# Values on quarters of the array in a first attention layer, and a new order of issue around the sixth and seventh steps of a second

## Time and profile before

| | us |
|---|---|
| median of 3 runs | 925.53 |
| lowest, highest | 922.88, 928.38 |
| the profiled execution | 926.4 |
| its span, first to last instruction | 924.6 |
| PE busy in it | 881.2 (95%) |
| DVE, ACT, POOL busy | 513.5, 511.7, 374.0 |

### The profile page before, as it was taken

One profiled execution on the slowest core, in us unless ns is written; L12 is line 12 of the kernel. 1 busy time (PEld: TensorE's weight loads), 2 busy tenths in 40 slices (PEclk: granted clock), 3 DMA queues, 4 the chain that ended last, 5 costly groups with the idle time before them and its releaser, 6 DMA issues.

```text
span 924.6 us, 20158 instructions
## 1 busy us (share of the span) xinstructions
PE 881.2 (95%) x6773; PEld 764.1 (83%) x6774; DVE 513.5 (56%) x1257; ACT 511.7 (55%) x1450; POOL 374.0 (40%) x530
## 2 busy tenths in 40 slices
PE   6989999999999999999999987999999999999996
PEld 4567777777777779999999986899999999987653
DVE  4534434444445764434434447877777776666466
ACT  4576777777775244443343462655655555552565
POOL 3173444444443234455454551534434443443000
PEclk9999999999999799999999998999999999999998
DMA  9000000420002466777777813000000000000002
GB/s 267 1 1 2 1 1 2 146 72 1 0 2 80 138 240 234 244 245 258 232 262 246 252 61 89 25 23 13 12 23 11 12 1 2 1 1 0 1 1 91
DMA packets 36673, 76.18 MB, mean 82 GB/s; under 512 B 4941, under 2 KB 22721, under 8 KB 36481
## 3 DMA queue, kind: packets, MB, share of 16 engines
q1 hardware_dynamic: 32865, 65.11, 21.6%
q0 software_dynamic: 3744, 10.23, 3.3%
HBM read 66.02 MB, written 9.31 MB: 81 GB/s over the span
## 4 chain that ended last, share of the span: by engine, by line
PE 88%; DVE 4%; DMA 3%; issue 2%; ACT 1%; POOL 1%; SPq 0%; DVEq 0%; POOLq 0%
PE banks L1542 14%; PE banks L546 14%; PE banks L548 13%; PE banks L547 13%; PE banks L584 8%; PE banks L595 7%; PE banks L574 5%; PE banks L444 3%; PE banks L1827 2%; PE banks L515 1%; PE banks L1838 1%; PE banks L1832 1%; PE banks L1820 1%; PE banks L1532 1%; DMA region_a<-in_L_ffn_b 1%
## 5 line engine op out<-in xcount | busy, mean ns | idle before, releaser
L1098 ACT ACTIVATE region_a<-banks,negmax 128x154 f32<-128x154 f32 (+1 forms) x384 | 161.7, 434 | 29.3 <-DVE negmax L890 26.6
L1542 PE MATMUL banks<-region_b,region_a 128*128 128x128 f32 x1248 | 146.7, 276 | 1.5 <-ACT region_b L1578 1.4
L1542 PEld LDWEIGHTS banks<-region_b,region_a 128*128 128x128 f32 x1248 | 142.7, 192 | 3.2 <-ACT region_b L1578 1.7
L1242 POOL TENSOR_TENSOR region_a<-region_a,recip 128x640 f32<-128x640 f32 x64 | 80.3, 1255 | 137.4 <-DVE recip L894 137.4
L1205 POOL TENSOR_TENSOR region_a<-region_a,recip 128x512 f32<-128x512 f32 x64 | 66.7, 1042 | 134.3 <-DVE recip L894 94.9
L890 DVE TENSOR_REDUCE negmax<-banks 128x4 f32<-128x616 f32 (+1 forms) x128 | 100.5, 785 | 26.9 <-PE banks L574 14.2
L1633 DVE SCALAR_TENSOR_TENSOR region_b<-banks,region_a,region_b 128x128 f32<-128x128 f32 x156 | 43.9, 343 | 106.7 <-PE banks L1542 99.6
L584 PE MATMUL banks<-ident,region_a 128*128 128x128 f32 x640 | 95.0, 279 | 3.2 <-DVE pT_low L901 1.6
L584 PEld LDWEIGHTS banks<-ident,region_a 128*128 128x128 f32 x640 | 72.5, 141 | 16.6 <-issue 11.6
L546 PE MATMUL banks<-xT_high,Wq_high 128*128 128x256 f32 x256 | 77.8, 304 | 4.1 <-DVE xT_low L882 2.1
L1080 ACT CAST pT_high<-banks 128x640 fp32r<-128x640 f32 x64 | 44.4, 694 | 64.9 <-PE banks L584 64.9
(11 more groups left out here) (293 smaller groups left out, 2344.5 us busy)
## 6 DMA issues: line engine op xcount, KB each, us to landing
region_a<-in_L_ffn_W SPq DMA_DIRECT2D x39, 1024.0 KB
W<-in_L_ffn_W SPq DMA_DIRECT2D x1, 4096.0 KB, 17.9
W<-y_rows SPq DMA_DIRECT2D x16, 256.0 KB, 2.8
out<-x SPq DMA_DIRECT2D x8, 256.0 KB, 2.2
x<-in_x SPq DMA_DIRECT2D x1, 1536.0 KB, 13.1
region_b<-in_L_xattn_Wq SPq DMA_DIRECT2D x1, 1024.0 KB, 8.7
region_b<-in_L_xattn_Wo SPq DMA_DIRECT2D x1, 1024.0 KB, 13.6
xn_rows<-region_b SPq DMA_DIRECT2D x1, 1024.0 KB, 4.4
```

The lines of the kernel that those rows point to most:

```text
L1098: e = act.activation(into, source, ACT.Exp, bias=negmax[:, n % 2, u:u + 1], accum_out=sums[:, n % 2, u:u + 1])
L1242: pool.tensor_tensor(probs1[:, n % 2], probs1[:, n % 2], rc, ALU.mult).then_inc(sem("p_norm"), 1)
L1542: mm = pe.matmul(banks[:, 2 * r + part, m * P:(m + 1) * P], W1[r][:, k, cols], xgT[:, r, k, :], start=(k == 0), stop=(k == DK - 1))
```

## The change

For the first layer (L0):

- the values of a whole group are issued at the even step, and none at the odd one. Keys beyond 128 are no longer multiplied with zero rows: the four products (two heads' halves, two chunks) take 64 rows by 64 columns each, a quarter of the array, and the two row halves write to different banks, 5 and 6, columns 128 to 383 (`o0_ps`);
- ACT copies the group from the banks to SBUF (`o0T`), and DVE makes both high and low part from there. PE waits for `o0_copied` in place of `o2_sb`, and, as bank 5 is shared with the fifth transposed block, before that fifth transpose at odd steps; before the values it waits until ACT has copied this step's transposes;
- both output products lie in one bank, side by side in bank 7, and `add_y` for both comes at step 5;
- the next pair's rows are transposed to `o0_ps`, without a wait for `y_done`; the fifth transpose of step 6 waits for `xt2_sb`; `y_done` is awaited ahead of the queries.

For the second layer (L1):

- `pe_pair_x`, with its wait for `y_done`, comes behind `next_scores(6)` instead of ahead of it; ACT and DVE take its copies at the start of step 6;
- `values(6)` is issued ahead of the queries of step 6, and `values(7)` ahead of `next_scores(7)` and the queries of step 7.

```diff
+        o0_ps = banks[:, 5:7, P:P + PAIR]
...
-        def pe_pair_probsT(pe, L, n):
+        def pe_pair_probsT(pe, L, n, groups_copied=None, rows_split=None):
             row = normed if L is L0 else probs_row[:, n % 2]
             for m in range(5):
+                if m == 4 and groups_copied is not None:
+                    pe.wait_ge(sem("o0_copied"), groups_copied)
+                if m == 4 and rows_split is not None:
+                    pe.wait_ge(sem("xt2_sb"), rows_split)
...
+        def pe_group_values(pe, g, b):
+
+            V = V0[b].bitcast(F32)
+            for u in range(2):
+                for i in range(2):
+                    pe.matmul(o0_ps[64 * i:64 * i + 64, u, :], V[:, 2 * g + u, 128 * i:128 * i + 64], p0T[:, g % 2, 2 * u + i, :],
+                              start=True, stop=False)
+            for i in range(2):
+                for u in range(2):
+                    rows = slice(64 * u, 64 * u + 64)
+                    mm = pe.matmul(o0_ps[64 * i:64 * i + 64, u, :], V[rows, 2 * g + u, 192 + 64 * i:256 + 64 * i],
+                                   p0T[rows, g % 2, 4, :], start=False, stop=True)
+            mm.then_inc(sem("o2_ps"), 1)
...
+                if L is L0 and r == 0 and c % 2 == 0:
+                    pe.wait_ge(sem("o2_sb"), groups_done - (NC - 2 - c) // 2)
...
                 def values(n):
                     s = 8 * i + n
+                    if L is L0:
+                        if n % 2 == 0 and not (first and n in (0, 2)):
+                            pe.wait_ge(sem(probs_turned), s)
+                            if not (first and n == 4):
+                                pe.wait_ge(sem("o0_copied"), group + n // 2 - 2)
+                            pe_group_values(pe, (n // 2 - 2) % 4, before if n < 3 else batch)
+                        return
...
                 values(5)
-                if not last:
+                if not last and L is L0:
+                    pe.wait_ge(sem("pt2_high"), 8 * i + 5)
+                    pe.wait_ge(sem("xn_ready"), 2 * i + 4)
+                    pe_pair_x(pe, L)
+
+                next_scores(6)
+                if not last and L is L1:
                     if first:
                         pe.wait_ge(sem("q2_sb"), g0 + 4)
                     else:
                         pe.wait_ge(sem("y_done"), t0 + 2 * i)
                     pe.wait_ge(sem("xn_ready"), t0 + 2 * i + 4)
                     pe_pair_x(pe, L)
-
-                next_scores(6)
                 transposes(6)
...
+                if L is L1:
+                    values(6)
                 if not last:
                     pe.wait_ge(sem("xt2_sb"), x0 + i + 2)
+                    if L is L0:
+                        if first:
+                            pe.wait_ge(sem("q2_sb"), 4)
+                        else:
+                            pe.wait_ge(sem("y_done"), 2 * i)
                     pe_pair_q(pe, L, 0)
-                values(6)
+                if L is L0:
+                    values(6)
 
                 transposes(7)
...
+                if L is L1:
+                    values(7)
                 next_scores(7)
                 if not last:
                     pe.wait_ge(sem("q2_sb"), g0 + 4 * i + 5)
                     pe_pair_q(pe, L, 1)
-                values(7)
+                if L is L0:
+                    values(7)
...
             def o_rest(g, group):
                 high, low = oT_parts[L.index]
                 part = slice(2 * g, 2 * g + 2)
+                if L is L0:
+                    dve.wait_ge(sem("o0_copied"), group + 1)
+                    dve.tensor_copy(high[:, part, :], o0T).then_inc(sem("o2_high"), 1)
                 dve.wait_ge(sem("o2_high"), g0 + group + 1)
-                dve.tensor_tensor(low[:, part, :], o_ps.rearrange("p (u n) -> p u n", u=2),
+                dve.tensor_tensor(low[:, part, :], o0T if L is L0 else o_ps.rearrange("p (u n) -> p u n", u=2),
                                   high[:, part, :].bitcast(F32), ALU.subtract).then_inc(sem("o2_sb"), 1)
...
+                    if L is L1 and n == 6 and not last:
+                        pair_x_rest(i + 2)
                     if not (first and n == 0):
                         probsT_rest((n - 1) % 8, s - 1)
+                    if L is L0 and n % 2 == 1 and not (first and n in (1, 3)):
+                        o_rest((n // 2 - 2) % 4, 4 * i + n // 2 - 2)
...
-                    if n in (3, 5) and not first:
+                    if n in (3, 5) and not first and L is L1:
                         add_y(dve, L, 2 * i + n // 2 - 3, n // 2 - 1, misc_ps[:, 0:D])
-                    if n == 5 and not last:
+                    if n == 5 and not first and L is L0:
+                        dve.wait_ge(sem("y_ps"), 2 * i)
+                        for q in range(2):
+                            add_y(dve, L, 2 * i + q - 2, q, misc_ps[:, q * D:(q + 1) * D])
+                    if L is L0 and n == 5 and not last:
                         pair_x_rest(i + 2)
...
             def o_high(g, group):
                 act.wait_ge(sem("o2_ps"), g0 + group + 1)
+                if L is L0:
+                    if not (isinstance(group, int) and group == 0):
+                        act.wait_ge(sem("o2_sb"), group)
+                    act.copy(o0T, o0_ps).then_inc(sem("o0_copied"), 1)
+                    return
...
+                    if L is L1 and n == 6 and not last:
+                        x_high(i + 2)
                     if not (first and n == 0):
                         probsT_high((n - 1) % 8, s - 1)
```

More of the change, by code:

```diff
@@ L665, in transposes @@
                             pe.wait_ge(sem(probs_turned), s - 1)
-                        pe_pair_probsT(pe, L, (n - 1) % 8)
+                        turned = L is L0 and n % 2 == 1 and not (first and n < 5)
+                        pe_pair_probsT(pe, L, (n - 1) % 8, 4 * i + n // 2 - 1 if turned else None,
+                                       i + 2 if L is L0 and n == 6 and not last else None)
                 def next_scores(n):
@@ L712, in emit @@
                 transposes(3)
-                if not first:
+                if not first and L is L0:
+                    pe_pair_out(pe, L, 1, misc_ps[:, D:2 * D], range(0, 4), 4 * i, True)
+                elif not first:
                     pe_pair_out(pe, L, 0, misc_ps, range(4, NC), 4 * i)
@@ L718, in emit @@
                 transposes(4)
-                if not first:
+                if not first and L is L0:
+                    pe_pair_out(pe, L, 0, misc_ps, range(4, NC), 4 * i)
+                elif not first:
                     pe.wait_ge(sem("y_done"), t0 + 2 * i - 1)
@@ L1015, in emit @@
                         pair_q_rest(4 * i + n - 1, n - 6)
-                    if n % 2 == 0 and not (first and n in (0, 2)):
+                    if L is L1 and n % 2 == 0 and not (first and n == 0 or first and n == 2):
                         o_rest((n // 2 - 2) % 4, 4 * i + n // 2 - 2)
```

78 lines of the change are left out of this document (41 added, 37 removed).

## The result

The changed kernel took 932.39 us (median of 20 runs, 929.99 to 938.05), the kernel before beside it 927.31 (20 runs, 922.88 to 934.02). The ratio is 1.0063 with a 95% interval of 1.0048 to 1.0079: some 6 us slower. The forecast was 933.0. The profiled execution of the changed kernel has a span of 931.6 us, against 924.6 before.

The account below looks back on a forecast made before the run. PE was taken to bound both attention loops, idle only 1.2 of 189.0 and 3.6 of 228.0 us. First layer -4.3 and second +11.7 gave +7.4 on 926.4: 933.8, 933 for the median; range 920 to 944.

Parts of the forecast that it names:

- values(7) waits for the output group: Second layer, step 7: ACT copies queries before the output group, so PE stalls 1.85 us in each pair.
- Second layer, queries of step 0: Second layer: queries of step 0 wait for the low part of step 7's queries, a stall of 0.66 us.
- What goes there: Second layer: waits for y_done (0.7) and xt2_sb (0.25) vanish, together -0.95 us for each of 6 pairs.
- The layer: Second layer's sum: net +1.56 per pair, six pairs +9.4, first pair +2.3, last pair 0: +11.7 us.
- The group on quarters: First layer: a group's values take 1.58 us instead of 2.03, four quarters at once; 30 groups give -13.5 us.
- The rival of two at a time: First layer: quarters run only two at a time, 2.00 us per group, total 945.5; chance 0.12.
- The waits that come in the first layer: First layer's new stalls: next rows +4.9, step 7 +1.7, query copies +2.8, first pair +0.5, POOL's rows +1 us.
- The waits that go in the first layer: First layer: PE's waits for y_done and xt2_sb go, -1.7 us over seven pairs at most.
- The layer's sum, -4.3: First layer's total: -13.5 - 1.7 + 4.9 + 1.7 + 2.8 + 0.5 + 1 = -4.3 us.
- Rival 1: First layer: ACT and DVE keep up, so the new waits cost nothing; total 922.5, not slower; chance 0.27.
- rival 2: Second layer: values(7) waits for nothing, the new order does what it suggests; total 915; chance 0.10.
- rival 4: First layer: DVE's SBUF operations hold up POOL's normalisation at each odd step, 0.4 x 28; total 943; chance 0.10.

Follow-up runs that it names:

- l1_only: Kernel before with only the second layer's new order, first layer as before: 937.76 us, ratio 1.0118.
- group_first: Changed kernel, but at step 6 of the second layer ACT and DVE copy the output group ahead of the queries: 923.33 us, ratio 0.9962.
- q1_early: group_first plus ACT's copy of the second queries ahead of the exponentials at step 7 of the second layer: 915.82 us, ratio 0.99.
- full_rows: Changed kernel with the first layer's remaining-key products on all 128 rows again, still in one visit: 941.62 us, ratio 1.0166.
- l0_only: Changed kernel with the second layer in its old order, so only the first layer's part of the change: 925.07 us, ratio 0.9983.
- warm: l0_only with fifteen products of ones in PE's idle places of the first layer's first and last pairs: 919.25 us, ratio 0.9934.
- before_warm: Kernel before with the same fifteen products of ones in the first layer's first and last pairs: 927.98 us, ratio 1.0016.
- after_warm: Changed kernel, both layers as changed, with the same fifteen products of ones: 934.04 us, ratio 1.0061.
- best: Changed kernel with the edits of q1_early and warm, and the first layer's high copy of the output group on ACT: 919.03 us, ratio 0.9893.

## Why the prediction held

- **Second layer, values(7) waits for the output group.** Predicted 1.85 in each pair, measured 1.79; l1_only shows it without the first layer's edits, group_first removes it by order alone.
- **Second layer, queries of step 0.** Predicted 0.66, measured 0.67; q1_early removes it.
- **What goes there.** 0.95 a pair was taken, measured 1.12: before the change the values of step 5 took 1.92 to the next rows' transposes where 1.05 is unhindered, so the wait for the addition was up to 0.87 and not the 0.7 of the view of waits, and 0.25 for `xT_low`. Net the pair grew by 1.3 (32.71 to 34.00) where 1.56 was predicted. q1_early brings it to 0.66 under before and not to 1.12, because 0.23 at step 7 and 0.25 at step 0 are left.
- **The layer.** Predicted 11.7, in the profiles 12.2, of which 11.0 is the order and 1.2 the clock; 10.9 in l1_only's times. The 11.0 are seven stalls as predicted, but shared otherwise: five pairs at 1.3 to 1.4 and the last two stalls at 2.1 each, since five pairs' rows had waited for the addition and the prediction took six.
- **The group on quarters.** Predicted 1.58, measured 1.60; four at once, which no row had shown. The rival of two at a time (945.5) is close to what full_rows runs as, 941.6. Over 30 groups the 0.43 gives -12.9 where -13.5 was taken.

The Trainium skill, TensorEngine Tiling (Array Packing), Key Properties, has different tiles run in parallel; these rows agree with it for four 64x64 tiles, which the trace before left open.

- **The waits that come in the first layer.** Next rows at step 6, fifth transpose 90.91 and query 91.01, where transposes to query is otherwise 0.52: 1.06 - 0.52 = 0.54 (predicted 0.7). Step 7, from the transposes to the scores, 1.03 against 0.70 in the kernel before: 0.34 (0.25). Queries of step 0, transposes 67.01 to queries 67.75, 0.74 against 0.52: 0.22 (0.2); but the output product of step 2, the other of the two places, waited for nothing, so that term, 14 times 0.2, was twice too large. POOL's rows late at two odd steps, scores to transposes 0.88 against 0.73, 0.16 each, 2.2 in seven pairs (1). The rows of three of these:

```profile
73.83 0.79 PE L581 MATMUL banks<-region_a 64*128 64x154 f32 x8
74.71 0.44 PE L595 MATMUL banks<-ident,region_a 128*128 128x128 f32 x2
...
90.91 0.33 PE L595 MATMUL banks<-ident,region_a 128*128 128x128 f32 x1 [0.31 <-DVE xT_low L938]
91.01 0.36 PE L550 MATMUL banks<-xT_high,Wq_high 128*128 128x256 f32 x1
...
94.22 1.10 PE L595 MATMUL banks<-ident,region_a 128*128 128x128 f32 x5
95.25 0.40 PE L581 MATMUL banks<-region_a 64*128 64x154 f32 x2
```

- **The waits that go in the first layer.** Before the change the transposes of step 6 took 0.75 to the queries, 0.23 over unhindered: 1.6 in seven pairs (predicted 1.7). What the prediction did not have is 0.16 a pair at the next rows' transposes, which now follow the output product directly (its start to theirs is 1.51, where it was 1.61 to the values; theirs to the scores is 0.53, where it was 0.59).

All of it adds up to the pair's -0.66: four groups -1.70, then -0.23 and -0.16, and the new waits of 0.54, 0.34, 0.22 and twice 0.16. The layer's sum, -4.3, was right in the trace (-4.4) in part by luck: two terms too large (4.9 for 3.8, 2.8 for 1.5) and two too small (1.7 for 2.4, 1 for 2.2) cancelled. The total has luck too. The layers' +7.8 in the profiles holds 1.2 of the clock, and the median came within 1 us of the forecast 933.0 although the difference was smaller than forecast, 5 to 6 us and not 7.4, because the kernel before itself took 927.31 beside it and not 925.53.

- **Rival 1** (the covers hold) falls by these four waits, **rival 2** (values wait for nothing) is what group_first and q1_early had to build by hand, **rival 4** (POOL held up everywhere) was real in its mechanism and small in its price.

So the single traces add up to +7.8 and the medians to +5.1 (ratio 1.0063, 4.4 to 7.3 in us of before). By the times alone the first layer's -4.4 is hard to see: -1.6 in l0_only, -5.1 from l1_only to the changed kernel, -7.6 between the two kernels with products of ones. The clocks on record explain most of the scatter. Within one kernel the time changes by 0.61 us for each 0.001 of mean granted clock (from the 167 executions that have both on record). With it, as an estimate, every kernel's mean can be brought to one clock, 0.987, and set against the kernel before in its own series; an error of 0.5 to 0.8 us remains. Beside it stands what the traces give: -4.4, from the changed kernel's profile, wherever the new first layer is in, and the second layer's difference in length, without what the clock took in its first stretch.

| | traces | times at one clock |
|---|---|---|
| l0_only | -4.4 | -3.7 |
| l1_only | +10.9 | +11.6 |
| changed kernel | +6.6 | +6 (against all three series) |
| group_first | -4.2 | -4.4 |
| q1_early | -7.2 | -8.5 |

So the first layer's gain does arrive, and the two parts add up in the times as in the traces. warm comes to -4.3, no more than 0.6 from l0_only: what it had gained over it was in the main the clock. before_warm comes to +2.3 and after_warm to +8.2, both some 2 us slower for the products; why warm is not is open.

The fall of the clock is shown to have cost one execution of l0_only 7.7 us; what makes it fall is open. The changed kernel and q1_early idled in the same places as l0_only and kept the clock there. Of the eight profiles with the new first layer and no products, five fell to 0.50 in the first pair (from 51.9 to 53.1 on), and of the three with products none did; in the last steps best fell in spite of them, and l1_only fell with the old first layer (6.8 us from 287.0 on). Filling the places lowered the time of one kernel in three.

## What to carry over

When PE's order of issue is changed, change the order of the copies behind it on ACT and DVE with it: here two copies in the old order cost 9 us in the medians (10.8 in the traces, without the clock), and turning these round, with one more copy moved ahead of the exponentials, made a slower kernel 1% faster than the original. Follow each moved operation to the engine that frees its buffer, and count from that engine's queue, not from PE's. Where two engines' steps become unequal (2.8 and 4.6 us here), work that a later engine spreads evenly comes late in the short step.

## What the hardware showed that was not expected

- Four 64x64 fp32 products in four quarters ran at once: eight records of 256 columns in 0.59 us to the next scores, where eight of 128x64 took 1.02. Their records start in fours, the first four between 70.39 and 70.41, the second between 70.66 and 70.68; those of full_rows in twos.
- DVE and POOL held each other up, and the one that began first did not always end first. DVE before POOL by 0.08 in the earlier trace rows ended last; here DVE's copy, also 0.08 ahead, took its own 0.42, and POOL's multiplication 1.23 in place of 1.04; then DVE's subtraction with both inputs in SBUF took 1.41, twice the 0.69 of those that read a bank, and POOL's short one 0.84 in place of 0.41. Over the layer 22 of the 32 subtractions took 1.41, seven 1.11 and three 0.69, while all 32 copies took 0.42 or 0.43:

```profile
87.49 0.42 DVE L964 CAST o0T_high<-region_a 128x512 fp32r<-128x512 f32 x1
...
87.57 1.23 POOL L1279 TENSOR_TENSOR region_a<-region_a,recip 128x512 f32<-128x512 f32 x1 [3.06 <-PE banks L595]
...
87.94 1.41 DVE L966 TENSOR_TENSOR o0T_low<-region_a,o0T_high 128x512 fp32r<-128x512 f32 x1
...
88.77 0.84 POOL L1281 TENSOR_TENSOR region_a<-region_a,recip 128x128 f32<-128x128 f32 x1
```

The Trainium skill, SBUF — State Buffer, section "SBUF: two separate sides", says that an operation of DVE with two SBUF inputs and one of GpSimd exclude each other, and that the one that starts first holds the port for its whole instruction. These rows agree with the first, in both directions; the earlier trace rows, where DVE began first and ended last, does not agree with the second, at least by the starts on record. The loss came to PE as 0.16 us twice a pair, not as the 0.4 at every odd step that rival 4 feared.

- One program, two clocks: with the same first layer the last steps took 22.9 us in l0_only, with 17.1 us at a granted clock of 0.50, and 16.6 in q1_early. Single profiles of this kernel can differ by 7 us for that reason alone, as much as the whole change; so read the clock of each stretch ahead of its length, and compare executions at like clocks.
